# Cross-attention block: projections of the next batch moved into the attention steps

## What is computed

```python
x = layer_norm(hidden_states, ln1_w, ln1_b)
q = (x @ q_w + q_b).reshape(B, LQ, H, HD).transpose(0, 2, 1, 3)
k = (encoder_hidden_states @ k_w + k_b).reshape(B, LK, H, HD).transpose(0, 2, 1, 3)
v = (encoder_hidden_states @ v_w + v_b).reshape(B, LK, H, HD).transpose(0, 2, 1, 3)
scores = jnp.einsum('bhqd,bhkd->bhqk', q, k) * scale
scores = jnp.where(mask, scores, mask_value)
attn = jax.nn.softmax(scores, axis=-1)
out = jnp.einsum('bhqk,bhkd->bhqd', attn, v).transpose(0, 2, 1, 3).reshape(B, LQ, D)
hidden = out @ cproj_w + cproj_b + hidden_states
y = layer_norm(hidden, ln2_w, ln2_b)
y = jax.nn.gelu(y @ fc_w + fc_b, approximate=True)
return hidden + y @ proj_w + proj_b
```

## Time and profile before

| | |
|---|---|
| median of 3 runs | 886.25 us (881.57 to 886.69) |
| profiled execution | 884.75 us, span 883.0 us |
| busy, share of the span | PE 90%, DVE 51%, ACT 31%, POOL 36% |
| mean granted TensorE clock | 0.965 of full speed |
| DMA moved | 85.38 MB |

### The profile page before, as it was taken

One profiled execution on the slowest core, in us unless ns is written; L12 is line 12 of the kernel. 1 busy time (PEld: TensorE's weight loads), 2 busy tenths in 40 slices (PEclk: granted clock), 3 DMA queues, 4 the chain that ended last, 5 costly groups with the idle time before them and its releaser, 6 DMA issues.

```text
span 883.0 us, 9704 instructions
## 1 busy us (share of the span) xinstructions
PE 797.6 (90%) x3728; PEld 562.0 (64%) x3728; DVE 447.6 (51%) x711; ACT 276.1 (31%) x483; POOL 313.9 (36%) x190
## 2 busy tenths in 40 slices
PE   7898792963799999999999889999999999999998
PEld 5786571842344454454445268888888888888886
DVE  6815331432587668976877973553333333233222
ACT  4432131112567546536653620011111211121110
POOL 1724121000479638636983753542200120012000
PEclk9999896995899999999999999999999999999999
DMA  7342424443345354416542214410400040002001
GB/s 286 124 172 102 174 103 149 151 152 134 91 121 145 85 155 122 111 59 179 153 114 87 69 61 155 134 45 1 143 1 1 0 143 1 1 1 95 1 1 48
DMA packets 42605, 85.38 MB, mean 97 GB/s; under 512 B 4064, under 2 KB 12516, under 8 KB 39488
## 3 DMA queue, kind: packets, MB, share of 16 engines
q1 hardware_dynamic: 42416, 84.75, 29.9%
q10 hardware_dynamic: 144, 0.02, 0.0%
HBM read 59.45 MB, written 25.18 MB: 96 GB/s over the span
## 4 chain that ended last, share of the span: by engine, by line
PE 63%; DMA 16%; DVE 14%; SPq 3%; issue 2%; ACT 1%; POOL 0%; ACTq 0%; DVEq 0%; POOLq 0%
PE ps L383 16%; PE ps L385 15%; PE ps L384 15%; DMA ks<-BIG 8%; DVE mx L859 5%; PE ps L483 5%; PE ps L499 5%; PE ps L468 4%; PE ps L514 3%; SPq L222 2%; DMA qs<-BIG 2%; DMA R<-in_cproj_w 2%; DVE BIG L899 1%; DMA RAWY<-in_x 1%; DMA BIG<-mk 1%
## 5 line engine op out<-in xcount | busy, mean ns | idle before, releaser
L1123 POOL TENSOR_TENSOR R<-Pt 128x1024 f32<-128x1024 f32 x59 | 143.9, 2458 | 168.7 <-ACT Pt L692 88.4
L859 DVE TENSOR_REDUCE mx<-ps 128x1 f32<-128x512 f32 x256 | 162.8, 680 | 62.9 <-PE ps L468 62.8
L692 ACT ACTIVATE Pt<-ps 128x512 f32<-128x512 f32 x256 | 135.0, 600 | 113.8 <-PE ps L483 110.8
L483 PE MATMUL ps<-BIG 98*128 98x512 f32 x256 | 100.4, 437 | 25.8 <-DMA BIG<-mT 18.4
L468 PE MATMUL ps<-BIG 97*128 97x512 f32 x256 | 96.1, 418 | 29.3 <-DMA BIG<-mk 17.0
L1012 DVE CAST HR<-R 128x512 fp32r<-128x512 f32 x52 | 24.3, 467 | 184.6 <-ACT R L726 184.6
L483 PEld LDWEIGHTS ps<-BIG 98*128 98x128 f32 x256 | 44.5, 193 | 94.6 <-ACT Pt L692 42.4
L726 ACT ACTIVATE R<-ps,cols 128x512 f32<-128x512 f32 x52 | 35.9, 690 | 205.4 <-PE ps L385 205.4
L468 PEld LDWEIGHTS ps<-BIG 97*128 97x128 f32 x256 | 49.5, 194 | 52.6 <-DVE mx L859 25.3
L383 PE MATMUL ps<-BIG,HR 128*128 128x512 f32 x192 | 75.4, 393 | 2.3 <-DVE HR L1014 2.3
L383 PE MATMUL ps<-YT,BIG 128*128 128x512 f32 x192 | 75.9, 395 | 0.0
(11 more groups left out here) (107 smaller groups left out, 1329.7 us busy)
## 6 DMA issues: line engine op xcount, KB each, us to landing
ks<-BIG SPq DMA_DIRECT2D x32, 256.0 KB
qs<-BIG SPq DMA_DIRECT2D x32, 256.0 KB
BIG<-qs SPq DMA_DIRECT2D x16, 512.0 KB
BIG<-ks SPq DMA_DIRECT2D x16, 512.0 KB
R<-hd SPq DMA_DIRECT2D x28, 256.0 KB, 4.3
BIG<-qs SPq DMA_DIRECT2D x16, 256.0 KB
BIG<-ks SPq DMA_DIRECT2D x16, 256.0 KB
R<-in_x SPq DMA_DIRECT2D x16, 256.0 KB, 4.4
```

What stands on the lines that cost most here:

```text
L483: eng.matmul(bk, K_[0:98, j, kc * 128:(kc + 1) * 128], Q_[0:98, j, :], start=True, stop=True).then_inc(S["p_ra"], 1)
L692: eng.activation(Pt[:, r, j % 2, :], bank(3 + place % 3), ACT.Exp, scale=SCALE).then_inc(S["a_ra"], 1)
L859: eng.tensor_reduce(mx[:, s % 2, 4 * j + qc:4 * j + qc + 1], bank(place % 3), AX.X, ALU.max).then_inc(S["v_rb"], 1)
L1123: eng.tensor_tensor(R0[:, 2 * hp:2 * hp + 2, :], Pt[:, (r - 2) % 6, :, :], Pt[:, r, :, :], ALU.add).then_inc(S["g_ac"], 1)
```

## The change

Only batch 0's K, Q and V and batch 1's Q stay ahead of the steps (`FIRST`). Each other unit, and the output projections of batches 0 to 2, is given to one attention step (`BESIDE`): in it the unit's 12 products are issued in four chunks of three, between the step's score products. Units go through two banks of their own, so the rings of `s1` and `s2` have two banks each (three from step 56 on). The turns of x of batches 2 and 3, and of the first feed-forward input, take one place each in a step (`TURNS`).

SBUF has no room for all weights: v_w and c_w take turns in one place (`W2`), loaded and split again for each batch, q_w and k_w of batches 2 and 3 come in pieces of 128 columns (`load_piece`, `piece_high`, `piece_low`), and there is one place for the context, loaded again when the last V unit of the batch before is done. Q and K units in the steps have two `QK` places. Maxima are stored by a DMA that ScalarE issues, right behind its own copy, in place of SyncE. K comes first in the front part, ahead of Q and V. `add_bias` follows the output projection in place of preceding it.

The diff, cut to its core: the two tables, the rings, then SyncE's front order and step loop, TensorE's, ScalarE's, VectorE's and GpSimd's.

```diff
+        FIRST = [(kind, 0, g) for kind in "kqv" for g in range(4)] + [("q", 1, g) for g in range(4)]
+        BESIDE = [None] * NI
+        for g in range(4):
+            BESIDE[2 * g + 1] = ("k", 1, g)
+            BESIDE[12 + g] = ("v", 1, g)
+            for b in (1, 2):
+                BESIDE[16 * b + g] = ("q", b + 1, g)
+                BESIDE[16 * b + (5, 9, 10, 11)[g]] = ("k", b + 1, g)
+                BESIDE[16 * b + 12 + g] = ("v", b + 1, g)
+                BESIDE[16 * b + (4, 6, 7, 8)[g]] = ("c", b - 1, g)
+            BESIDE[52 + g] = ("c", 2, g)
...
+            def ra(key, late=False):
+                put(key, (0, 1, 4)[len(RA) % 3] if late else len(RA) % 2, ("a_ra", len(RA) + 1))
...
+            def rb(key, late=False):
+                put(key, (2, 3, 5)[len(RB) % 3] if late else 2 + len(RB) % 2, ("v_rb", len(RB) + 1))
...
+            def load_piece(u):
...
+                eng.dma_start(hl[2], kp(k_w if kind == "k" else q_w)[:, :, g * 128:(g + 1) * 128]).then_inc(S[name], 16)
...
+            load_x(0)
+            load_weights(q_w, WQ, "d_wq")
+            load_weights(v_w, WV0, "d_wv")
             sp.wait_ge("v_mf", 2)
             eng.dma_start(mk, R2[0:4, 1, :]).then_inc(S["d_mk"], 16)
             sp.wait_ge("cst", 3)
             eng.dma_start(on.rearrange("a (p c) -> (a p) c", c=32), ones[0:16, :]).then_inc(S["d_on"], 16)
+            load_x(1)
+            for g in range(4):
+                store_qk(("k", 0, g))
+            for g in range(4):
+                store_qk(("q", 0, g))
+                if g < 3:
+                    load_stack(g)
             eng.dma_start(cbt[:, :], c_b.partition_broadcast(128)).then_inc(S["d_cb"], 16)
-            sp.wait_ge("v_lo", 9)
-            sp.wait_ge("g_lo", 1)
-            load_raw(2, xv[1], 2)
-            for b in range(B):
-                if b == 3:
-                    load_stack(1)
-                for g in range(4):
-                    store_qk(b, g, 0)
-                if b == 2:
-                    load_stack(0)
-                if b == 0:
-                    sp.wait_ge("p_tr", 4)
-                    load_raw(3, cv[2], 2)
-                if b == 1:
-                    sp.wait_ge("g_lo", 5)
-                    load_raw(1, cv[3], 2)
-                    sp.wait_ge("p_tr", 8)
-                    load_raw(2, xv[3], 2)
-                if b == 3:
-                    load_stack(2)
-                for g in range(4):
-                    if b == 3 and g == 2:
-                        store_max(0)
-                    store_qk(b, g, 1)
-                    if b == 0 and g == 1:
-                        sp.wait_ge("g_lo", 3)
-                        load_raw(0, xv[2], 2)
-            sp.wait_ge("g_xl", 16)
-            eng.dma_start(R2[:, :, :], kp(c_w)).then_inc(S["d_wc"], 16)
+            load_context(1)
+            for g in range(4):
+                store_qk(("q", 1, g))
+            load_x(2)
...
                 if kc == 0 and s >= 1 and s + 2 < NS:
                     load_stack(s + 2)
+                if t == 0 and b:
+                    sp.wait_ge(*made(("v", b, 3)))
+                    load_weights(c_w, W2, "d_wc")
+                    if b < 3:
+                        load_context(b + 1)
+                if i and BESIDE[i - 1] and BESIDE[i - 1][0] in "kq":
+                    store_qk(BESIDE[i - 1])
+                if t == 2 and b:
+                    load_residual(b - 1)
+                if b in (1, 2):
+                    if t == 3:
+                        load_piece(("k", b + 1, 0))
+                    if t == 4:
+                        for g in range(1, 4):
+                            load_piece(("k", b + 1, g))
+                if i >= 3 and BESIDE[i - 3] and BESIDE[i - 3][0] == "c":
+                    store_hidden(*BESIDE[i - 3][1:])
+                if b < 2:
+                    if t == 6:
+                        load_piece(("q", b + 2, 2))
+                    if t == 10:
+                        load_piece(("q", b + 2, 3))
+                    if t == 12:
+                        load_piece(("q", b + 2, 0))
+                        load_piece(("q", b + 2, 1))
+                if i == 8 or (b in (1, 2) and t == 9):
+                    sp.wait_ge(*made(("c", b - 1, 3) if b else ("k", 1, 3)))
+                    load_weights(v_w, W2, "d_wv")
+                if i == 14:
+                    load_x(3)
+                if i == 30:
                     ln2_load(0)
+                if i == 58:
+                    load_residual(3)
...
+            for k in range(4):
+                for g in range(4):
+                    product(("k", 0, g), k)
+            for k in range(4):
+                x_turn(0, k)
+            for k in range(4):
+                product(("q", 0, 0), k)
+                product(("q", 0, 1), k)
+            for g in (2, 3):
+                for k in range(4):
+                    product(("q", 0, g), k)
+            x_turn(1, 0)
+            x_turn(1, 1)
+            for k in range(4):
+                product(("v", 0, 0), k)
+                if k % 2:
+                    x_turn(1, 2 + k // 2)
+            for k in range(4):
+                product(("v", 0, 1), k)
+            for c in (2, 3):
+                for k in range(4):
+                    product(("v", 0, c), k)
+                    s1(4 * (c - 2) + k)
+            for g in range(4):
+                for k in range(4):
+                    product(("q", 1, g), k)
+                    s1(8 + 4 * g + k)
+                if g == 2:
+                    turn_maxima(0)
 
 
             for i in range(NI):
                 s, kc = divmod(i, 4)
+                u = BESIDE[i]
                 s2(i, 0)
                 s2(i, 1)
+                if u:
+                    product(u, 0)
                 for m in range(4):
+                    if m in (1, 2):
+                        s2(i, m + 1)
+                    if m == 3 and i in TURNS:
+                        if TURNS[i][0] == "xt":
+                            x_turn(*TURNS[i][1:])
+                        else:
+                            pe.wait_ge("v_nm", 20)
+                            y_turn(0, TURNS[i][2], psum(TURNS[i])).then_inc(S["p_rb"], 1)
                     tile, turn = MAXIMA[4 * i + m]
                     if tile is not None:
                         s1(tile)
                     if turn is not None:
                         turn_maxima(turn)
+                    if m == 0 and i:
+                        pv(i - 1)
+                    if m == 2:
+                        if kc == 3:
+                            sums(s, 1)
+                        if kc == 1 and s:
+                            sums(s - 1, 3)
+                    if u and m < 3:
+                        product(u, m + 1)
...
+                if q >= 3:
+                    act.wait_ge(*last_s2(q - 3))
+                act.wait_ge("a_ra", RA[("mt", q)] + 1)
+                eng.dma_start(STK[q % 3][0].bitcast(F32)[97:98, :, :], mT[:, :].bitcast(F32)).then_inc(S["d_m"], 16)
...
+            for k in range(4):
+                context_high(0, k)
+            for k in range(4):
+                weights_high(WQ, k, 0, "d_wq", "a_wq")
+            for k in range(4):
+                x_high(0, k)
+            for g in range(4):
+                qk_high(("k", 0, g))
+            for k in range(4):
+                weights_high(WV0, k, 0, "d_wv", "a_wv")
+            for g in range(4):
+                qk_high(("q", 0, g))
+            x_high(1, 0)
+            x_high(1, 1)
+            x_high(1, 2)
+            copy_v(("v", 0, 0))
+            x_high(1, 3)
+            for c in range(1, 4):
+                copy_v(("v", 0, c))
+            qk_high(("q", 1, 0))
+            qk_high(("q", 1, 1))
+            context_high(1, 0)
+            context_high(1, 1)
+            copy_maxima(0)
+            qk_high(("q", 1, 2))
+            context_high(1, 2)
+            context_high(1, 3)
+            qk_high(("q", 1, 3))
...
+                if b and t in (1, 2):
+                    for k in (2 * t - 2, 2 * t - 1):
+                        weights_high(W2, k, b - 1, "d_wc", "a_wc")
+                if b in (1, 2) and t in (2, 3):
+                    for k in (2 * t - 4, 2 * t - 3):
+                        context_high(b + 1, k)
+                if b < 3 and t - (b > 0) in (9, 10):
+                    k = 2 * (t - (b > 0) - 9)
+                    weights_high(W2, k, b + 1, "d_wv", "a_wv")
+                    weights_high(W2, k + 1, b + 1, "d_wv", "a_wv")
+                if b in (1, 2) and 4 <= t < 8:
+                    piece_high(("k", b + 1, t - 4))
+                if b < 2 and t >= 12:
+                    piece_high(("q", b + 2, (2, 3, 0, 1)[t - 12]))
...
+                    if m == 0 and u and u[0] in "kq":
+                        qk_low(u)
+                    if m == 0 and u and u[0] == "c":
+                        residual(u)
...
+                if b < 3:
+                    n = b + 2
```

(28 more changed lines are left out.)

842 lines of the change are left out of this document (400 added, 442 removed).

## The result

The kernel after takes 919.04 us (median; 916.82 to 922.62), the kernel before on the same chip 886.47 (881.57 to 887.94). The ratio is 1.038, 95% interval 1.033 to 1.043: slower by 3.8%, where 874 was forecast with 902 as the upper end. The profiled execution has a span of 917.8 us; the sum gave 872.5.

A forecast was written before the change was run, and what follows sets the result against it. The prediction took the first stage to be bound by K and Q stores, the attention by TensorE. Front 97, clock 2.5, attention 363, waits 36 and feed-forward 374 sum to 872.5 us of span, so 874, range 848 to 902.

The forecast's parts named there:

- First step starts, clock with it: Front: SyncE's chain of stores and loads lets the first step start at 97 us, plus 2.5 for the slow clock.
- Attention, undisturbed steps: Attention if nothing waits: 270 us as before, 90 for 32 added products, 3 for eight turns of x; 363 us.
- Steps 2 and 3, the x load: VectorE waits for batch 2's x, loaded behind eight Q stores: 7 us and 2 for the clock, 9.
- Steps 10 to 12, v_w: ScalarE waits for v_w behind a stack load and a K store pair, in steps without a product: 4 us.
- Two-bank rings and the last steps: Attention: 8 us for two-bank rings, 5 idle in its last 72 us, 3 for late maxima at a short step.
- the clock: TensorE's lower clock behind long waits: 2.5 us charged at the front and 2 behind the x wait.
- the ring's 0.6: Two-bank rings cost 0.6 us in each of 14 attention steps without a product that still make maxima: 8 us.
- None is the bound: Attention: VectorE, ScalarE and GpSimd, at 75, 69 and 75 of 105 us a batch, have room for extra splits.
- 3.5 each: Steps 21 and 37: the K product waits for its weight's low half behind GpSimd's other work; 7 us together.
- stores on the other queue do hold them up: Rival: stores delay the maxima on ScalarE's queue, up to 9 us at the front; 890 us, chance 0.10.
- The one that foresaw a slower kernel (904): Rival: reloads and stores fill the DMA queue and pace batches 1 and 2, 15 us each; chance 0.22.
- The turning point: The change turns from faster to slower where the sum of stalls passes 49 us.

The follow-up runs named there:

- a_x2: Kernel after with the load of batch 2's x issued ahead of the eight Q stores of batch 1 on SyncE's queue; 912.29 us.
- a_split: Kernel after with each K or Q store written as four DMAs, one for each head; 892.43 us, ratio 1.006.
- b_ring2: Kernel before with score rings of two PSUM banks in place of three; 921.64 us, ratio 1.040.
- a_int: Kernel after with VectorE's extra splits and norms issued one at a time between the maxima, not two together at a step's end; 910.96 us.
- a_gp: Kernel after with GpSimd's sums of exponentials cut to 16 of 512 columns in each half; 898.83 us.
- a_ord: Kernel after with GpSimd's low half of the K weight put ahead of that step's context splits and root; 909.63 us.
- a_k6: Kernel after with the K product of step 5 of batches 1 and 2 moved to step 6, output projections shifted to match; 908.05 us.
- a_warm: Kernel after with 22 matrix products on ready data put ahead of the K product of steps 21 and 37, waits unchanged; 915.26 us.
- a_lay_all: Kernel after with the edits of b_lay, a_k6 and a_int together; 852.40 us, ratio 0.962.
- b_lay: Kernel before with the K and Q scratch laid out head by head, a store being one DMA of 128 rows; 825.81 us, ratio 0.932.

## Why the prediction was wrong

Point by point, the forecast against the profile:

| Term | Forecast | Measured |
|---|---|---|
| First step starts, clock with it | 97 + 2.5 | 104.6 |
| Attention, undisturbed steps | 363 | 366.5 |
| Steps 2 and 3, the x load | 9 | 10.8 |
| Steps 6 and 7, norms | 0 | 6.4 |
| Steps 10 to 12, v_w | 4 | 10.6 |
| Steps 19 to 23, K weight | 3.5 | 11.8 |
| Steps 35 to 39, the same | 3.5 | 10.9 |
| Steps 27 to 31, 43 to 47, 52 to 55 | 0 | 12.8 |
| Two-bank rings and the last steps | 16 | 12.2 |
| All other steps | 0 | -2.8 |
| Feed-forward | 374 | 374.0 |

The measured column sums to 917.8, the forecast's to 872.5. The rows of waits are what each group of steps takes over its undisturbed time, so a row also holds what the clock and the two-bank rings cost there.

**Right.** That stores bound the front, at 2.45 us each; that nothing moves behind the attention; the product's 2.73 us (a step of 3.18 takes 5.85 with one, a step of 3.28 5.88); the price and the place of the x wait (a_x2: 9.1) and of the wait for v_w (a_split: 3.0 in step 10, 4 forecast); the ring's 0.6 (b_ring2). The averages were right as well: over each of batches 1 and 2 VectorE is busy for 81 and 80 us (75 forecast), ScalarE for 63 and 59 (69) and GpSimd for 74 and 68 (75). What was concluded from them was not.

**The step that failed** is "None is the bound, so extra splits cost nothing on average; what hides them is the product beside them." An average over a batch of 105 us says nothing of a single gap between two maxima. The splits and norms stood two together at a step's end, each of them can stand until a GpSimd instruction has ended, and the maxima that free the second ring's two banks come behind them: a block of up to 4.9 us (481.19, two subtractions), where a product hides 2.73. That is the 6.4 of steps 6 and 7 and some 5 of steps 10 to 12, and part of the 12.8 (1.6 of it is step 45, which no other profile repeats; how much of the rest belongs here is not shown). a_int takes 8.1 us away by the order alone, 3.6 of it in steps 6 and 7 and 4.0 in steps 10 to 12; a_gp takes 5.0 from steps 6 and 7 with GpSimd nearly empty. The trace of the kernel before had the price already, in the four norms that stand in its attention, which took 2.12 us each; in the kernel after two of them take 0.96 together where GpSimd is idle (154.55):

```profile
L818 DVE TENSOR_SCALAR HN<-HN,mv,rs 128x512 f32<-128x512 f32 x4 | 8.5, 2116 | 0.0
```

**The second** is "3.5 each" for steps 21 and 37. The chain had the right members and the right length (12.9 us from 243.95 to 256.86, 13 forecast) and the wrong start. It was counted from the second exponential of step 19, which ended at 241.30; but the sums write the tile `R0`, which TensorE's ones-product at the end of step 19 still reads, and began 2.65 us later. The earlier trace rows had already named that releaser for 80.2 us of their idle time. So the wait became 5.60 us, and the clock behind it made 8 of it. a_ord and a_k6 put the price of the two steps at 9 to 11 us.

**The third** is the clock. It was charged once at the front (2.5) and 2 in step 1. a_warm shows that a wait of 5.6 us costs 2.35 and 1.51 more behind it, 42 and 27% of itself, and the profile after has 43.9 us of idle time in the attention. The forecast, with the rings' 8 us counted as busy, had 371 busy and 28 idle; measured are 395.3 and 43.9. In that attention TensorE was busy for some 43 us at a granted clock of 0.50, where the products follow each other at 0.43 us and not at 0.23; at full clock the same work takes some 20 us less, most of the 24 that were not forecast. In a_lay_all, with half of the idle time gone, only 17 us are busy at 0.50, which would take 12 us of busy time away; 16 are gone. These sums are estimates from the profiles; an experiment that changes the clock alone was made only for steps 21 and 37.

**The front** missed by 5, mostly at its start. The first store was issued at 27.17 (26 forecast), and the load of stack 0, which waits for the landing of ten stores, at 57.36 (51.0):

```profile
27.17 13.50 SPq L340 DMA_DIRECT2D ks<-YT  x8
...
57.36 0.50 SPq L356 DMA_DIRECT2D BIG<-qs  x1
```

Ten stores at 2.45 us are 24.5; from the first issue to that landing it was 30.2. From there the loads were 13.1 us apart (13.8 forecast), and ScalarE began the context split at 97.95, where 93.4 was reckoned. The maxima behind it took 4.42 us to land on ScalarE's queue (99.43 to 103.84), where the forecast took 1.8 from below and had 11.2 from above; over all 16 the median is 4.3:

```profile
BIG<-mT ACTq DMA_DIRECT2D x16, 8.0 KB, 4.3
```

So stores on the other queue do hold them up, by 2.6 us at the front. It cost little, since TensorE had three matrix products and a score tile to do until 104.56, and no later wait of TensorE in the attention is for the maxima.

**The rivals.** The one that foresaw a slower kernel (904) had the direction right by luck, for the wrong reason. a_split shows middle batches that don't care for the queue, and what that rival would have shown is absent: ScalarE stood 2.6 us at a weight piece in each middle batch, not over 10. The turning point that it gave, stalls of 49 us, holds: they came to 73. TensorE was busy for 92% between steps 16 and 47, not over 95, and they took 242.7 us, not 215.

## What to carry to other kernels

When operations are moved in between others, price them by the gap that they must fit, in the queue where they stand, and at the duration they have beside the engine that then runs; a batch's average hides both. When a stage is bound by one kind of transfer, ask first what it costs to mend the transfer where it is: b_lay saved 60 us with the layout of the two scratch tensors, and left 10 us of idle time in the first stage for the rearrangement to win. Where a TensorE wait lasts several us, add something for the clock behind it; the two of 5.6 us here cost three and four tenths on top.

## What the runs showed of the hardware

- Some VectorE operations stand while GpSimd works on SBUF, until the GpSimd instruction that they met has ended. Two subtractions with both inputs in SBUF take 1.25 us alone and 4.17 beside two sums; two norms from SBUF 0.99 (a_gp) and 3.58. All 22 that met a GpSimd instruction in the attention of the kernel after ended at a fixed distance behind its end, 0.55 us for a subtraction and 0.28 to 0.29 for a norm. The maxima, which read PSUM, have 0.69 in both cases, and so have the batch-norm statistics (0.68), although they read SBUF. GpSimd gives up less: two sums take 4.89 us with the norms between them and 5.22 with the subtractions, where the median of one is 2.39. The Trainium skill (Perfetto Trace Analysis, Optimizing Scalar/DVE Operations) says that the two engines share an SBUF read port, which agrees with the rows of the subtractions and norms. The same section of the Trainium skill says that breaking up instructions may help where an engine that isn't saturated causes bubbles. No run here breaks one up: a_int only issues the same instructions one at a time, which saved 8.1 us.
- Useless work in TensorE's idle time can pay: 22 products in a wait of 5.6 us saved 2.35 us behind it in step 21 and 1.51 in step 37.
- Two rings one bank shorter cost 36 us of attention in the kernel before (b_ring2), of which TensorE's idle time shows 4.
- 8 KB issued on ScalarE's queue landed in 1.76 to 6.0 us in the kernel after, 1.8 in the median of the kernel before on SyncE's queue.
